# First layer's recurrence on one core: values and gates formed ahead for all tokens, fetched per step by a selection product, temporaries in PSUM, turns of 64 steps

## The chip, the cores and the metric

One core of a Trainium2 chip runs a ten-layer model in one launch. The metric is the device time of the whole launch in microseconds, the median of several executions. The change lies in the first layer, named "cells".

## What is computed

The first layer is a gated matrix recurrence over 1024 tokens of 4 sequences. After x is projected to 128 features, each token gives, for four blocks of 32, a key, a value, a gate (beta), routing logits and one query. The step over time is:

```python
def step(S, inp):                       # S: (batch, 4 blocks, 32, 32)
    logits_t, k_t, v_t, beta_t, q_t = inp
    ...                                 # w: weights of the top 2 of 4 blocks
    kn = k_t / (jnp.linalg.norm(k_t, axis=-1, keepdims=True) + 1e-06)
    retrieved = jnp.einsum('bnij,bnj->bni', S, kn)
    delta = v_t - retrieved
    outer = delta[..., :, None] * kn[..., None, :]
    S_upd = jnp.tanh(beta_t[..., None] * S + outer)
    S_new = (1.0 - w) * S + w * S_upd
    Sq = jnp.einsum('bnij,bj->bni', S_new, q_t)
```

Each step needs the state of the step before, so the 1024 steps run one after another. The other nine layers (a coupling net, a linear recurrence, a binary product, a gated scan, an fp4 feed-forward, RWKV, and local attention in three parts) are not touched.

## The kernel before, in words

The engines run five separate instruction streams, tied by one counting semaphore per layer and engine; `e.after(label)` is a wait for the operation that was recorded with `e.did(label)`, and `back=1` means that operation's instance in the previous turn. Each stream is in order, so the order of the code is the order of the work on that engine.

State. S of one step is a tile of 128 partitions (4 sequences x 32 values of j) by 128 columns (4 blocks x 32 values of i), held in `big7` in two copies used in turn. The sum over j of the delta rule goes over the 32 partitions of a sequence, so it is a product with a constant matrix, `negblock32`, on TensorE. S is never multiplied by the next key after it is complete. Its two parts are: S_new times next key is (1-w) next key S, called kS and made by GpSimd from the state before, plus (w next key) tanh(arg), called kT and made by VectorE from tanh.

Per step s the streams do this.
- TensorE, `cells_tensor`, lines 504 to 544: kS product (L510) and kT product (L514) are added to the bank of step s, in which the value product of the step already stands; then the read-out of the state before (L501), the value product of the next step (L471), one logits product for the gates (L481; every fourth step also a bias product, L479), and a bf16 product whose result nobody reads (L543). Float32 products show as two matmul records and two weight loads each.
- VectorE, `cells_vector`, L770 to L825: outer = bank x key (L775), arg = outer + bS (L778), kT (L811) and wT (L812) from tanh, the new S = wT + aS (L820), bS = S x gate of the next step (L825). bS, outer, arg, T, wT and aS are tiles of `big7`, 128 x 128 float32. Between arg and kT it copies keys, weights, queries and read-outs of half a turn in small pieces, one in each of steps 1 to 7 and 17 to 23 (L724 to L750).
- ScalarE, `cells_scalar`, L598 to L615: tanh (L604); every fourth step it repeats four steps' tokens 32 times over the columns (`repeat_x`, L588), which is the stationary operand of the value and logits products, and makes the gates of four steps by sigmoid (L614).
- GpSimd, `cells_pool`, L873 to L891: kS (L882) and aS (L883), both as soon as the S of the step before is there.

The loop is unrolled by 32 steps, with 32 turns. Products of steps alternate between banks 0 and 2, the gates' logits between banks 5 and 6, the read-outs of half a turn lie in banks 4 and 7. Ahead of the loop VectorE works out routing weights and normed keys (L633 to L713), then ScalarE forms the first turn's repeated tokens and gates (L591 to L597). "staged" is the label of the memset at L713 that frees `big7` for the state.

Of the kernel before, what the change touches and what calls it, by code (L numbers as in the profile page):

```python
# [21 lines left out]
ALU = mybir.AluOpType  # L22
# [130 lines left out]
STEPS = 32  # L153
PARTS = 1
HALF_STEPS = STEPS // 2
CELL_TURNS = SEQ // STEPS
NB = BLK // PARTS
HALF = NB * NST
# [109 lines left out]
class Core:  # L268


    def __init__(self, nc, ctx, ins, out, places, known, found, layers):
# [9 lines left out]
        self.b = [sb(f"big{n}", [P, TOK + (BATCH * STEPS if n == 0 else 0)]) for n in range(9)]  # L281
# [129 lines left out]
def cells_buffers(core):  # L411
    b = core.b
    st = core.b[7]
    cut = lambda a, n: st[:, a:a + n]
    return dict(
        xp=b[0], kn=b[1], wt=b[2], knext=b[3], qd=b[4], lg=b[5], ex=b[6], tmp=b[7], sq=b[8],
        xrep=b[5].rearrange("p (s c) -> p s c", c=P), beta=b[6].rearrange("p (s c) -> p s c", c=P),
        kn_c=cut(0, 128).rearrange("p (n s) -> p n s", n=4), w_c=cut(128, 128).rearrange("p (n s) -> p n s", n=4),
        om_c=cut(256, 128).rearrange("p (n s) -> p n s", n=4), qd_c=cut(384, 128),
        S=[cut(512, 128), cut(640, 128)], aS=cut(768, 128), bS=cut(896, 128), kT=cut(1024, 128),  # L420
        kS=[cut(1664, 128), cut(1792, 128)],
        **{k: cut(at, 128).rearrange("p (n s) -> p n s", n=4) for k, at in (("kw_c", 1920), ("ko_c", 2048), ("knext_c", 2176))},
        outer=cut(1152, 128), arg=cut(1280, 128), T=cut(1408, 128), wT=cut(1536, 128),
        out_bank=[core.bank[4], core.bank[7]],
    )
# [12 lines left out]
def cells_tensor(core, e):  # L438
# [24 lines left out]

    G = STEPS // 4
    logit_bank = [core.bank[5], core.bank[6]]

    def values(s, label):


        for h in range(PARTS):  # L470
            mm = nc.tensor.matmul(core.bank[s % 2 * 2 + h][:, 0:HALF], u["xrep"][:, s, :], w("wv", h * HALF, HALF),  # L471
                                  start=True, stop=False, skip_group_check=True)
        mm.then_inc(*e.did(label))

    def logits(g, m):

        bank = logit_bank[g % 2]
        if m == 0:
            nc.tensor.matmul(bank, core.half[:, TILE:TILE + P], core.half[:, 0:TILE], start=True, stop=False,  # L479
                             skip_group_check=True)  # L480
        return nc.tensor.matmul(bank[:, m * P:(m + 1) * P], u["xrep"][:, 4 * g + m, :], w("wbeta"),  # L481
                                start=False, stop=m == 3, skip_group_check=True)


    pe.wait_ge(*e.after("staged"))
    pe.wait_ge(*e.after("lexp"))
    for g in range(G):
        pe.wait_ge(*e.after("xrep0", g))
        if g >= 2:
            pe.wait_ge(*e.after("beta0", g - 2))  # L490
        for m in range(4):
            mm = logits(g, m)
        mm.then_inc(*e.did(("logits0", g)))
    pe.wait_ge(*e.after("beta0", G - 1))
    pe.wait_ge(*e.after("coefficients"))
    values(0, ("v0",))
# [6 lines left out]

    with e.turns("time", SEQ // STEPS):
        for s in range(STEPS):

            at = lambda x, h: x[:, h * HALF:(h + 1) * HALF]
            pe.wait_ge(*(e.after("kS", s - 1) if s else e.after("kS", STEPS - 1, back=1)))
            for h in range(PARTS):
                nc.tensor.matmul(core.bank[s % 2 * 2 + h][:, 0:HALF], core.c("negblock32"),  # L510
                                 at(u["kS"][(s - 1) % 2], h), start=False, stop=False, skip_group_check=True)
            for h in range(PARTS):
                pe.wait_ge(*(e.after("kT", s - 1, h) if s else e.after("kT", STEPS - 1, h, back=1)))
                nc.tensor.matmul(core.bank[s % 2 * 2 + h][:, 0:HALF], core.c("negblock32"),  # L514
                                 at(u["kT"], h), start=False, stop=True,
                                 skip_group_check=True).then_inc(*e.did(("delta", s, h)))
            if s > 0:
                pe.wait_ge(*e.after("S", s - 1, PARTS - 1))
            else:
                pe.wait_ge(*e.after("S", STEPS - 1, PARTS - 1, back=1))  # L520
# [6 lines left out]
            read_out((s - 1) % STEPS, ("Sq", (s - 1) % STEPS))  # L527
            if s >= 1:
                pe.wait_ge(*e.after("outer", s - 1, PARTS - 1))
            else:  # L530
                pe.wait_ge(*e.after("outer", STEPS - 1, PARTS - 1, back=1))
            if (s + 1) % 4 == 0:
                pe.wait_ge(*(e.after("xrep", (s + 1) // 4, back=1) if s + 1 < STEPS else e.after("xrep", 0)))
            values((s + 1) % STEPS, ("v", (s + 1) % STEPS))

            g, m = (s // 4 - 1) % G, s % 4
            if m == 0:
                pe.wait_ge(*e.after("xrep", g, back=int(s < 4)))
                pe.wait_ge(*e.after("beta", (g - 2) % G, back=int(s < 8)))
            mm = logits(g, m)  # L540
            if m == 3:
                mm.then_inc(*e.did(("logits", g)))
            nc.tensor.matmul(core.bank[1][:, 0:2 * P], core.half[:, 0:P], core.half[:, 0:2 * P], start=True, stop=True,  # L543
                             skip_group_check=True)
    pe.wait_ge(*e.after("S", STEPS - 1, PARTS - 1))
    read_out(STEPS - 1, "Sq_last")

    for label in [("beta", G - 1), ("out_last",)]:
        pe.wait_ge(*e.after(*label))
# [14 lines left out]
def cells_scalar(core, e):  # L564
# [11 lines left out]
    for t in range(TILES):  # L576
        bank, label = core.drain(e, core.to_act)
        nc.scalar.activation(u["tmp"][:, tok(t)], bank, ACT.Sqrt).then_inc(*e.did(label))
        core.found.at[("cells", "knorm", t)] = core.found.at[("cells", *label)]
    act.wait_ge(*e.after("lmax"))  # L580
# [4 lines left out]
    def repeat_x(g, start, label, turn=None):  # L585
        src = u["xp"][:, start:start + TOK].rearrange("p (b t) -> p t b", b=BATCH)
        src = src[:, 0:4, :] if turn is None else src[:, bass.ds(turn * STEPS, 4), :]
        nc.scalar.activation(u["xrep"][:, 4 * g:4 * g + 4, :].rearrange("p s (b j) -> p s b j", b=BATCH),  # L588
                             src.unsqueeze(3).broadcast_to([P, 4, BATCH, 32]), ACT.Copy).then_inc(*e.did(label))

    for g in range(G):  # L591
        repeat_x(g, 4 * g, ("xrep0", g))
    for g in range(G):
        act.wait_ge(*e.after("logits0", g))
        nc.scalar.activation(u["beta"][:, 4 * g:4 * g + 4, :].rearrange("p s c -> p (s c)"),  # L595
                             core.bank[5 + g % 2], ACT.Sigmoid).then_inc(*e.did(("beta0", g)))
    nc.scalar.preload_act_table(ACT.Sigmoid)  # L597
    with e.turns("time", SEQ // STEPS) as turn:  # L598
        for s in range(STEPS):
            for h in range(PARTS):  # L600
                act.wait_ge(*e.after("arg", s, h))
                if s % 4 == 3 and h == PARTS - 1:
                    act.wait_ge(*(e.after("v", s)))
                nc.scalar.activation(u["T"][:, h * HALF:(h + 1) * HALF], u["arg"][:, h * HALF:(h + 1) * HALF],  # L604
                                     ACT.Tanh).then_inc(*e.did(("T", s, h)))
            if s % 4 == 3:

                g = s // 4
                repeat_x(g, STEPS + 4 * g, ("xrep", g), turn)
            if s % 4 == 0:  # L610
                g = (s // 4 - 2) % G
                act.wait_ge(*e.after("bS", 4 * g + 3, back=int(s < 8)))
                act.wait_ge(*e.after("logits", g, back=int(s < 4)))
                nc.scalar.activation(u["beta"][:, 4 * g:4 * g + 4, :].rearrange("p s c -> p (s c)"),  # L614
                                     core.bank[5 + g % 2], ACT.Sigmoid).then_inc(*e.did(("beta", g)))  # L615
    act.wait_ge(*e.after("out_last"))
    for t in range(TILES):
        nc.scalar.activation(u["tmp"][:, tok(t)], u["sq"][:, tok(t)], ACT.Sigmoid).then_inc(*e.did(("osig", t)))
# [7 lines left out]
def cells_vector(core, e):  # L626
    nc, dve, u = core.nc, e.eng, cells_buffers(core)
    tt, G = nc.vector.tensor_tensor, STEPS // 4
# [18 lines left out]
    nc.vector.memset(u["xp"][:, TOK:], 0.0).then_inc(*e.did("xp_pad"))  # L647
# [119 lines left out]
    with e.turns("time", CELL_TURNS) as turn:  # L767
        after, back_one = ((turn + 1) % CELL_TURNS) * STEPS, ((turn + CELL_TURNS - 1) % CELL_TURNS) * STEPS
        first, second = bass.ds(after, HALF_STEPS), bass.ds(turn * STEPS + HALF_STEPS, HALF_STEPS)
        for s in range(STEPS):  # L770
# [8 lines left out]
            if s == 1:  # L779
                copy_key(1, second)  # L780
# [2177 lines left out]
```

## Time and profile before

| | us |
|---|---|
| median of 3 runs | 9550.41 |
| lowest, highest | 9549.36, 9557.72 |
| the profiled execution, its own time | 9542.88 |
| its span in the profile | 9541.1 |
| TensorE busy (matmul) | 7287.1 (76%) |
| VectorE busy | 6764.2 (71%) |
| ScalarE busy | 3257.0 (34%) |
| GpSimd busy | 3224.7 (34%) |

In the rows below, times are microseconds from the start of the span unless marked ns. PE is TensorE's matmul, PEld its weight load, DVE VectorE, ACT ScalarE, POOL GpSimd. L775 is line 775 of the kernel. Full clock is PEclk 1 (2.4 GHz), half clock 0.5 (1.2 GHz). "banks" is PSUM, "big" the big tiles in SBUF. PEclk is the granted TensorE clock as a share of 2.4 GHz. The time of a group of instructions is its busy time; what it means for the span shows only in the order of time.

### The profile page before, as it was taken

The page shows a single profiled execution, that of the slowest core. Times are in us where ns is not written, and L with a number is a line of the kernel's source. Part 1 is how long each engine was busy: PE and PEld are TensorE (multiplying, and loading weights), DVE is VectorE, ACT ScalarE, POOL GpSimd, SP SyncE. Part 2 cuts the span into 40 slices and gives each one's busy share as a digit, 9 for nine tenths or more (in the row PEclk, how much of TensorE's full clock was granted, in tenths as well). Part 3 has the DMA queues.
Part 4 walks back from the last instruction along what each step waited for, and adds up shares of the span by engine and source line. Part 5 has one row for each costly group of instructions (what it writes and reads, how often), then busy time and mean ns, then how long its engine had stood idle before and what let it go on. Part 6 is the DMA issues. An engine that isn't in the chain of part 4 may idle for free. (4 is left out here: it accounts for less than half of the span.)

```text
span 9541.1 us, 245537 instructions
## 1 busy us (share of the span) xinstructions
PE 7287.1 (76%) x92569; PEld 4453.7 (47%) x92569; DVE 6764.2 (71%) x15000; ACT 3257.0 (34%) x5970; POOL 3224.7 (34%) x3982
## 2 busy tenths in 40 slices
PE   4888888888874826656845768888888888888887
PEld 3666666666621212223223345545455545454554
DVE  7777777777758475765485557777777777777776
ACT  2222222222243313223413334444444444444444
POOL 1333333333300000210040035555555555555553
PEclk7888888888887867656865779999999999999999
DMA  0000000000000000000000031111111111111111
GB/s 18 1 1 1 1 1 1 1 1 1 1 5 1 15 0 0 0 0 1 0 0 1 1 120 54 53 53 54 48 56 51 54 51 51 56 51 56 51 56 57
DMA packets 156976, 243.21 MB, mean 25 GB/s; under 512 B 21617, under 2 KB 136849, under 8 KB 150161
## 3 DMA queue, kind: packets, MB, share of 16 engines
q1 hardware_dynamic: 155920, 228.84, 7.8%
q8 instruction: 699, 11.45, 0.5%
q14 instruction: 357, 2.92, 0.1%
HBM read 187.06 MB, written 13.66 MB: 21 GB/s over the span
## 5 line engine op out<-in xcount | busy, mean ns | idle before, releaser
L2751 POOL TENSOR_TENSOR big<-big 128x512 f32<-128x512 f32 x776 | 1040.1, 1373 | 278.4 <-DMA big<-norms 270.7
L2741 POOL TENSOR_TENSOR big<-big 128x512 f32<-128x512 f32 x388 | 494.7, 1275 | 1819.8 <-DVE big L2583 1819.8
L882 POOL TENSOR_TENSOR big<-big 128x128 f32<-128x128 f32 x1024 | 518.3, 506 | 1569.7 <-DVE big L820 1567.4
L604 ACT ACTIVATE big<-big 128x128 f32<-128x128 f32 x1024 | 316.8, 309 | 1902.0 <-DVE big L778 1876.8
L1856 POOL TENSOR_TENSOR small<-big 128x480 f32<-128x480 f32 (+14 forms) x240 | 220.9, 954 | 2187.2 <-ACT big L1614 1866.5
L2158 PE MATMUL banks<-hidden,big 128*128 128x256 f32 x3104 | 828.9, 401 | 111.8 <-DVE big L2583 41.1
L514 PE MATMUL banks<-big,constants_on_chip 128*128 128x128 f32 x2048 | 533.3, 347 | 409.8 <-DVE big L811 408.2
L337 PE MATMUL banks<-big,constants_on_chip 128*128 128x512 f32 (+15 forms) x1088 | 533.5, 644 | 355.2 <-DVE big L1747 191.3
L337 PE MATMUL banks<-big,weights_even 128*128 128x512 f32 (+5 forms) x1152 | 620.5, 692 | 235.0 <-DVE big L1137 45.1
L2222 PE MATMUL banks<-big,hidden 128*32 128x512 f32 x6144 | 770.5, 600 | 4.1 <-ACT big L2473 4.1
L2201 PEld LDWEIGHTS banks<-big 32*32 32x32 f32 x49152 | 535.2, 103 | 471.8 <-issue 471.1
L2201 PE MATMUL banks<-big 32*32 32x64 f32 (+1 forms) x49152 | 659.3, 222 | 87.0 <-issue 86.8
L2158 PEld LDWEIGHTS banks<-hidden,big 128*128 128x128 f32 x3104 | 557.7, 193 | 295.3 <-issue 61.1
L2240 PE MATMUL banks<-big 128*32 128x128 f32 x12160 | 442.0, 301 | 292.6 <-DVE big L2628 274.2
L2473 ACT ACTIVATE big<-banks 128x512 f32<-128x512 f32 x768 | 456.1, 596 | 540.7 <-PE banks L2222 540.4
L514 PEld LDWEIGHTS banks<-big,constants_on_chip 128*128 128x128 f32 x2048 | 352.5, 215 | 564.1 <-DVE big L811 562.5
L2741 POOL TENSOR_TENSOR big<-small 128x512 f32<-128x512 f32 x388 | 498.1, 1284 | 211.8 <-DVE small L2583 211.8
L2240 PEld LDWEIGHTS banks<-big 128*32 128x32 f32 x12160 | 376.8, 121 | 395.2 <-issue 321.0
L471 PE MATMUL banks<-weights_even,big 128*128 128x128 f32 x2050 | 560.7, 361 | 0.7 <-ACT big L595 0.7
L337 PEld LDWEIGHTS banks<-big,constants_on_chip 128*128 128x128 f32 x1088 | 246.7, 252 | 640.8 <-DVE big L1747 215.1
L811 DVE TENSOR_TENSOR big<-big 128x128 f32<-128x128 f32 x1024 | 299.2, 292 | 329.9 <-ACT big L604 313.1
L778 DVE TENSOR_TENSOR big<-big 128x128 f32<-128x128 f32 x1024 | 498.1, 486 | 35.4
(349 smaller groups left out, 15896.3 us busy)
## 6 DMA issues: line engine op xcount, KB each, us to landing
big<-norms SPq DMA_DIRECT2D x776, 128.0 KB, 2.9
big<-qk SPq DMA_DIRECT2D x50, 512.0 KB, 4.8
big<-vo SPq DMA_DIRECT2D x25, 1024.0 KB, 5.8
weights_odd<-ffn SPq DMA_DIRECT2D x25, 537.5 KB, 4.6
hidden<-big SPq DMA_DIRECT2D x171, 64.0 KB, 12.9
hidden<-big SPq DMA_DIRECT2D x25, 256.0 KB, 3.8
hidden<-big SPq DMA_DIRECT2D x25, 255.8 KB, 4.0
big<-pairs SPq DMA_DIRECT2D x6, 1024.0 KB, 10.4
```

The lines of the kernel that those rows point to most:

```text
L337: mm = self.nc.tensor.matmul(bank[0:rows, 0:cols], w, x, start=n == 0, stop=n == len(pairs) - 1)
L471: mm = nc.tensor.matmul(core.bank[s % 2 * 2 + h][:, 0:HALF], u["xrep"][:, s, :], w("wv", h * HALF, HALF), start=True, stop=False, skip_gro ...
L514: nc.tensor.matmul(core.bank[s % 2 * 2 + h][:, 0:HALF], core.c("negblock32"), at(u["kT"], h), start=False, stop=True, skip_group_check=Tru ...
L778: tt(cut(u["arg"], h), cut(u["outer"], h), cut(u["bS"], h), ALU.add).then_inc(*e.did(("arg", s, h)))
L882: nc.gpsimd.tensor_tensor(full(u["kS"][s % 2]), full(S), by(u["ko_c"]), ALU.mult).then_inc(*e.did(("kS", s)))
L2158: mm = self.nc.tensor.matmul(bank[:, n * QTOK:(n + 1) * QTOK], u["w" + name.lower()][:, (2 * g + n) * P:(2 * g + n + 1) * P], u["xs"][:, a ...
L2201: mm = self.nc.tensor.matmul(place[b][32 * c:32 * c + 32, gi, win, skip:], Q[rows, g, half, at:at + WIN], K[rows, g, half, at + skip:at + ...
L2222: mm = self.nc.tensor.matmul(bank[32 * c:32 * c + 32, :], u["xs"][:, at:at + WIN], u["vo"][:, c], start=True, stop=True)
L2240: mm = self.nc.tensor.matmul(u["out_bank"][32 * win:32 * win + 32, jj * P:(jj + 1) * P], u["probT"][jj][:, 4 * g + win, n, :], u["slots"][ ...
L2473: self.nc.scalar.activation(u["slots"][(4 * n + win) % SLOTS], u["value_banks"][win % 2], ACT.Copy).then_inc(*e.did(("kept", f, jj, win)))
L2741: self.nc.gpsimd.tensor_tensor(dst, cos, sin, ALU.add).then_inc(*e.did(("turned_pair", f, name, g)))
L2751: self.nc.gpsimd.tensor_tensor(x, x, u["norms"][:, n, g].unsqueeze(1).broadcast_to([P, 2, QTOK]), ALU.mult).then_inc(*e.did(("scaled", f, ...
```

## The change

1. `STEPS` is 64: 16 turns.
2. Ahead of the loop TensorE forms values and gate logits of all 4096 tokens, 16 products of 32 tokens x 128 to a bank, eight banks of each. ScalarE copies the values to `big3` and the sigmoid of the logits to `big5`. The result has (sequence, 32 steps) on the partitions, one 128-column tile for each half turn.
3. ScalarE spreads the identity to `own` (128 x 4096 columns): for each of 32 steps a 128 x 128 matrix that picks that step's token of each sequence and repeats it over 32 partitions. In the loop one product of `own` and a half turn's values and gates, 256 columns side by side (`vb`), puts both into the bank of the step. It replaces the value product, the logits product, the bias product and the bf16 product L543, and `repeat_x` and the sigmoids in the loop.
4. VectorE multiplies S by the gate straight from columns 128 to 255 of the step's bank. TensorE waits for that multiplication ahead of the kS product.
5. outer and wT lie in bank 2, arg and T in bank 3.
6. The half-turn copies move from VectorE to ScalarE, behind the tanh of steps 2 to 8 and 34 to 40. Two small operations (1 - w, and w x next key) stay on VectorE.
7. The copy of the keys shifted by one token goes; ScalarE reads the keys themselves one column further.

```diff
-STEPS = 32
-PARTS = 1
+STEPS = 64
...
-        outer=cut(1152, 128), arg=cut(1280, 128), T=cut(1408, 128), wT=cut(1536, 128),
+        step_bank=core.bank[0:2], outer=core.bank[2][:, 0:128], wT=core.bank[2][:, 128:256],
+        arg=core.bank[3][:, 0:128], T=core.bank[3][:, 128:256], out_bank=[core.bank[4], core.bank[7]],
...
+    def all_tokens(bank, weight, g, start):
+        for m in range(4):
+            for b in range(BATCH):
+                at = b * SEQ + (4 * g + m) * HALF_STEPS
+                mm = nc.tensor.matmul(bank[32 * b:32 * b + 32, m * P:(m + 1) * P], u["xp"][:, at:at + HALF_STEPS], weight,
+                                      start=start, stop=True, skip_group_check=True)
+        return mm
...
+    def value_and_beta(s, label):
+        nc.tensor.matmul(u["step_bank"][s % 2][:, 0:2 * P], u["own"][:, s % HALF_STEPS, :], u["vb"][s // HALF_STEPS], start=True, stop=False, skip_group_check=True).then_inc(*e.did(label))
...
+            before, back = (s - 1) % STEPS, {} if s else {"back": 1}
+            bank = u["step_bank"][s % 2][:, 0:P]
+            pe.wait_ge(*e.after("kS", before, **back))
+            pe.wait_ge(*e.after("bS", s, **back))
+            nc.tensor.matmul(bank, core.c("negblock32"), u["kS"][before % 2], start=False, stop=False, skip_group_check=True)
+            pe.wait_ge(*e.after("kT", before, **back))
+            nc.tensor.matmul(bank, core.c("negblock32"), u["kT"], start=False, stop=True,
+                             skip_group_check=True).then_inc(*e.did(("delta", s)))
+            pe.wait_ge(*e.after("S", before, **back))
...
+            read_out(before, ("Sq", before))
+            pe.wait_ge(*e.after("outer", before, **back))
...
+            value_and_beta((s + 1) % STEPS, ("v", (s + 1) % STEPS))
...
+    ident = core.c("ident").rearrange("p (b s) -> p s b", b=BATCH).unsqueeze(3).broadcast_to([P, HALF_STEPS, BATCH, 32])
+    copy(u["own"].rearrange("p s (b j) -> p s b j", b=BATCH), ident, "own")
+    act.wait_ge(*e.after("beta_kept", TILES - 1))
+    copy(u["vb"][0][:, 0:P], u["v"][:, 0:P])
+    copy(u["vb"][0][:, P:2 * P], u["beta"][:, 0:P], "vb_first")
...
+            dve.wait_ge(*e.after("delta", s))
+            tt(cut(u["outer"]), cut(u["step_bank"][s % 2][:, 0:P]), spread(u["kn_c"], s), ALU.mult).then_inc(
+                *e.did(("outer", s)))
...
+            tt(u["arg"], u["outer"], u["bS"], ALU.add).then_inc(*e.did(("arg", s)))
...
+            tt(new, u["wT"], u["aS"], ALU.add).then_inc(*e.did(("S", s)))
+            dve.wait_ge(*e.after("v", ahead))
+            dve.wait_ge(*e.after("S", s))
+            tt(u["bS"], new, u["step_bank"][ahead % 2][:, P:2 * P], ALU.mult).then_inc(*e.did(("bS", ahead)))
```

## Rows read from the trace of the kernel before

**Rows 1.** Groups by line of the time loop: names, shapes, count, busy us, mean ns, idle.

```profile
L604 ACT ACTIVATE big<-big 128x128 f32<-128x128 f32 x1023 | 316.5, 309 | 1900.0 <-DVE big L778 1874.7 <-PE banks L471 14.7 <-PE banks L481 10.6
...
L811 DVE TENSOR_TENSOR big<-big 128x128 f32<-128x128 f32 x1023 | 298.9, 292 | 329.5 <-ACT big L604 312.6
...
L775 DVE TENSOR_TENSOR big<-banks,big 128x128 f32<-128x128 f32 x1024 | 291.6, 285 | 151.5 <-issue 85.2 <-PE banks L514 63.0
...
L775 DVE TENSOR_TENSOR big<-banks,big x1024: 281/283/293, 164.4 to 2639.2; 128x128 f32<-128x128 f32 x171
```

**Rows 2.** Timeline of one step at full clock: start us, duration us, engine, line.

```profile
1501.32 0.30 PEld L471 LDWEIGHTS banks<-weights_even,big 128*128 128x128 f32 x2
...
1501.54 0.30 PEld L481 LDWEIGHTS banks<-weights_even,big 128*128 128x128 f32 x2
1501.60 0.41 POOL L883 TENSOR_TENSOR big<-big 128x128 f32<-128x128 f32 x1
1501.61 0.54 DVE L778 TENSOR_TENSOR big<-big 128x128 f32<-128x128 f32 x1
...
1501.88 0.30 PEld L510 LDWEIGHTS banks<-big,constants_on_chip 128*128 128x128 f32 x2
...
1502.19 0.31 ACT L604 ACTIVATE big<-big 128x128 f32<-128x128 f32 x1 [1.50 <-DVE big L778]
1502.53 0.29 DVE L811 TENSOR_TENSOR big<-big 128x128 f32<-128x128 f32 x1 [0.38 <-ACT big L604]
1502.74 0.28 DVE L812 TENSOR_TENSOR big<-big 128x128 f32<-128x128 f32 x1
...
1502.88 0.49 PE L514 MATMUL banks<-big,constants_on_chip 128*128 128x128 f32 x2 [0.50 <-DVE big L811]
1503.06 0.29 DVE L820 TENSOR_TENSOR big<-big 128x128 f32<-128x128 f32 x1
1503.38 0.29 DVE L825 TENSOR_TENSOR big<-big 128x128 f32<-128x128 f32 x1
...
1503.59 0.28 DVE L775 TENSOR_TENSOR big<-banks,big 128x128 f32<-128x128 f32 x1
```

**Rows 3.** Stretches: us, busy of PE, PEld, DVE, ACT, POOL, then PEclk, DMA, GB/s.

```profile
50.00:149.00 99.00, 0.00 (x0) 0.00 (x0) 97.03 (x58) 3.62 (x1) 0.00 (x0) 0.50 0.00 0
...
400.00:2600.00 2200.00, 1803.47 (x10230) 1485.91 (x10231) 1683.47 (x5854) 509.29 (x1363) 814.01 (x1876) 0.87 0.00 1
...
4308.00:4350.00 42.00, 30.70 (x278) 20.09 (x277) 15.21 (x39) 11.00 (x25) 0.00 (x0) 0.50 0.00 0
```

**Rows 4.** Timeline of steps at half clock.

```profile
204.28 0.29 DVE L775 TENSOR_TENSOR big<-banks,big 128x128 f32<-128x128 f32 x1 [0.66 <-PE banks L514]
...
204.61 0.29 DVE L778 TENSOR_TENSOR big<-big 128x128 f32<-128x128 f32 x1
...
204.94 0.31 ACT L604 ACTIVATE big<-big 128x128 f32<-128x128 f32 x1 [2.00 <-DVE big L778]
...
205.32 0.55 PEld L510 LDWEIGHTS banks<-big,constants_on_chip 128*128 128x128 f32 x2
...
205.75 0.55 PEld L514 LDWEIGHTS banks<-big,constants_on_chip 128*128 128x128 f32 x2
...
243.19 0.80 PE L514 MATMUL banks<-big,constants_on_chip 128*128 128x128 f32 x2 [1.79 <-DVE big L811]
...
244.03 0.29 DVE L775 TENSOR_TENSOR big<-banks,big 128x128 f32<-128x128 f32 x1
```

**Rows 5.** Timeline of VectorE over the end of a turn.

```profile
238.67 0.29 DVE L825 TENSOR_TENSOR big<-big 128x128 f32<-128x128 f32 x1
241.85 0.29 DVE L775 TENSOR_TENSOR big<-banks,big 128x128 f32<-128x128 f32 x1 [2.89 <-issue]
```

**Rows 6.** Timeline ahead of the loop.

```profile
149.66 4.26 ACT L588 ACTIVATE big<-big 128x512 f32<-128x512 f32 x8 [67.80 <-DVE big L713]
...
164.43 0.29 DVE L775 TENSOR_TENSOR big<-banks,big 128x128 f32<-128x128 f32 x1 [11.25 <-PE banks L514]
```

More of the change, by code:

```diff
@@ L280, in __init__ @@
         self.x = sb("hidden", [P, TOK])
-        self.b = [sb(f"big{n}", [P, TOK + (BATCH * STEPS if n == 0 else 0)]) for n in range(9)]
+        self.b = [sb(f"big{n}", [P, TOK + int(n == 1)]) for n in range(9)]
         self.const_at, n = columns(constants())
@@ L462, in cells_tensor @@
         core.product(e, core.to_act, [(core.c("block32"), u["tmp"][:, tok(t)])])
[L464 to L482, printed above, removed]
@@ L485, in cells_tensor @@
[L485 to L488, printed above, removed]
-        if g >= 2:
[L490 to L496, printed above, removed]
+    for k in range(core.to_act.filled - 4, core.to_act.filled):
+        pe.wait_ge(*e.after("drained", "to_act", core.to_act.phase, k))
@@ new lines, in all_tokens @@
+    def all_tokens(bank, weight, g, start):
[5 more added lines that the diff above has]
+        return mm
+    for g in range(TILES):
+        if g >= 2:
+            pe.wait_ge(*e.after("v_kept", g - 2))
+        all_tokens(core.bank[g % 2], w("wv"), g, True).then_inc(*e.did(("v_all", g)))
@@ new lines, in cells_tensor @@
+    for g in range(TILES):
+        if g >= 2:
+            pe.wait_ge(*e.after("beta_kept", g - 2))
+        bank = core.bank[2 + g % 2]
+        nc.tensor.matmul(bank, core.half[:, TILE:TILE + P], core.half[:, 0:TILE], start=True, stop=False,
+                         skip_group_check=True)
+        all_tokens(bank, w("wbeta"), g, False).then_inc(*e.did(("beta_all", g)))
+    def value_and_beta(s, label):
+        nc.tensor.matmul(u["step_bank"][s % 2][:, 0:2 * P], u["own"][:, s % HALF_STEPS, :], u["vb"][s // HALF_STEPS], start=True, stop=False, skip_group_check=True).then_inc(*e.did(label))
@@ L502, in read_out @@
                          start=True, stop=True, skip_group_check=True).then_inc(*e.did(label))
-    with e.turns("time", SEQ // STEPS):
-        for s in range(STEPS):
[L507 to L520, printed above, removed]
+    pe.wait_ge(*e.after("vb_first"))
+    pe.wait_ge(*e.after("own"))
+    pe.wait_ge(*e.after("coefficients"))
+    value_and_beta(0, "v_first")
+    with e.turns("time", CELL_TURNS):
+        for s in range(STEPS):
+            before, back = (s - 1) % STEPS, {} if s else {"back": 1}
[7 more added lines that the diff above has]
+            pe.wait_ge(*e.after("S", before, **back))
             if s == 1:
@@ L526, in cells_tensor @@
                 pe.wait_ge(*e.after("out", 1))
[L527 to L545, printed above, removed]
+            read_out(before, ("Sq", before))
+            pe.wait_ge(*e.after("outer", before, **back))
+            if s + 1 == HALF_STEPS:
+                pe.wait_ge(*e.after("vb", 1))
+            if s + 1 == STEPS:
+                pe.wait_ge(*e.after("vb", 0))
+            value_and_beta((s + 1) % STEPS, ("v", (s + 1) % STEPS))
+    pe.wait_ge(*e.after("S", STEPS - 1))
     read_out(STEPS - 1, "Sq_last")
-    for label in [("beta", G - 1), ("out_last",)]:
-        pe.wait_ge(*e.after(*label))
+    pe.wait_ge(*e.after("bS", 0))
+    pe.wait_ge(*e.after("out_last"))
     for t in range(TILES):
@@ L579, in cells_scalar @@
         core.found.at[("cells", "knorm", t)] = core.found.at[("cells", *label)]
+    for g in range(TILES):
+        act.wait_ge(*e.after("v_all", g))
+        nc.scalar.activation(u["v"][:, tok(g)], core.bank[g % 2], ACT.Copy).then_inc(*e.did(("v_kept", g)))
     act.wait_ge(*e.after("lmax"))
     nc.scalar.activation(u["ex"][:, 0:TOK], u["lg"][:, 0:TOK], ACT.Exp).then_inc(*e.did("lexp"))
-    act.wait_ge(*e.after("staged"))
[L585 to L596, printed above, removed]
+    for g in range(TILES):
+        act.wait_ge(*e.after("beta_all", g))
+        if g == 0:
+            act.wait_ge(*e.after("lexp"))
+        nc.scalar.activation(u["beta"][:, tok(g)], core.bank[2 + g % 2], ACT.Sigmoid).then_inc(*e.did(("beta_kept", g)))
@@ L597, in cells_scalar @@
+    copy(u["vb"][0][:, P:2 * P], u["beta"][:, 0:P], "vb_first")
+    act.wait_ge(*e.after("coefficients"))
     nc.scalar.preload_act_table(ACT.Sigmoid)
-    with e.turns("time", SEQ // STEPS) as turn:
+    with e.turns("time", CELL_TURNS) as turn:
+        after, earlier_turn = ((turn + 1) % CELL_TURNS) * STEPS, ((turn + CELL_TURNS - 1) % CELL_TURNS) * STEPS
         for s in range(STEPS):
[L600 to L615, printed above, removed]
@@ new lines, in cells_scalar @@
+            act.wait_ge(*e.after("arg", s))
+            nc.scalar.activation(u["T"], u["arg"], ACT.Tanh).then_inc(*e.did(("T", s)))
+            h = 0 if s >= HALF_STEPS else 1
+            start = after if h == 0 else turn * STEPS + HALF_STEPS
+            chore = s % HALF_STEPS
+            if chore == 2:
+                copy_steps("w_c", "wt", h, start, ("w_c", h))
+            if chore == 3:
+                copy_steps("knext_c", "kn", h, start, ("knext_c", h))
+            if chore == 4:
+                copy_steps("kn_c", "kn", h, start, ("kn_c", h))
@@ new lines, in cells_scalar @@
+            if chore == 5:
+                act.wait_ge(*e.after("Sq", HALF_STEPS - 1 if h == 0 else STEPS - 1))
+                copy(u["qd_c"][:, h * P:(h + 1) * P], u["qd"][:, bass.ds(start * BATCH, P)], ("qd_c", h))
+            if chore == 6:
+                done = turn * STEPS if h == 0 else earlier_turn + HALF_STEPS
+                keep_out(h, bass.ds(done, HALF_STEPS), ("out", h))
+            if chore == 7:
+                act.wait_ge(*e.after("v", HALF_STEPS - 1 if h == 0 else STEPS - 1, **({"back": 1} if h else {})))
+                copy_tile("v", h, start * BATCH, None)
@@ L616, in cells_scalar @@
+            if chore == 8:
+                copy_tile("beta", h, start * BATCH, ("vb", h))
+    act.wait_ge(*e.after("Sq_last"))
+    keep_out(1, slice(SEQ - HALF_STEPS, SEQ), "out_last")
     act.wait_ge(*e.after("out_last"))
+    act.wait_ge(*e.after("bS", 0))
     for t in range(TILES):
@@ L757, in cells_vector @@
     weigh_next_key(0)
[L758 to L759 removed]
+    e.name_last("coefficients")
     chain()
[L762 to L825 removed]
@@ L874, in cells_pool @@
             S = u["S"][s % 2]
-            for h in range(PARTS):
-                pool.wait_ge(*(e.after("S", s - 1, h) if s else e.after("S", STEPS - 1, h, back=1)))
+            pool.wait_ge(*(e.after("S", s - 1) if s else e.after("S", STEPS - 1, back=1)))
             by = lambda v: v[:, :, s].unsqueeze(2).broadcast_to([P, BLK, NST])
```

167 lines of the change are left out of this document (59 added, 108 removed).

## Prediction

> **What bounds the kernel now.** I read the grouped instructions of the time loop first, then one step of it in order of time, then the granted clock by stretch, a low-clock step, the turn boundary and the stretch ahead of the loop. The loop is L775 to L825, 1024 steps; its first L775 starts at 164.4 us and its last at 2639.2 [rows 1], so it takes 2475 of 9541 us, 2.42 us a step. Nothing else is touched but some 15 us ahead of it.
>
> In a plain step [rows 2] VectorE is the chain. From start to start: kT L811 to wT L812 0.21 (2.53 to 2.74), to the new state S L820 0.32, to bS L825 0.32, to the next outer L775 0.21, to arg L778 0.32 (204.28 to 204.61 [rows 4]), to tanh on ScalarE L604 0.58 (1501.61 to 1502.19), and to kT 0.34: 2.30 us. TensorE's part lies beside it: L514 starts 0.34 after kT starts, its record takes 0.49 and ends at 1503.37, and L775 starts only at 1503.59, because VectorE was still making wT, S and bS. So TensorE has 0.2 us to spare. The earlier product of the sum, L510 on kS, ran at 1501.88, a microsecond ahead of kT. And L778, both inputs in SBUF, takes 0.54 beside GpSimd's L883, where L775, one input in PSUM, takes 0.28. Without GpSimd beside it L778 takes 0.29 (at 204.61), and ScalarE follows 0.33 after its start [rows 4].
>
> Check: 1023 x 2.30 = 2353; 31 turn ends add 3.18 - 0.21 = 2.97 each, less 0.25 for an L778 that runs with GpSimd still idle there [rows 5]: 84; the 38 us left of 2475 are steps at the lower TensorE clock, where TensorE's queue of products is the bound (L775 waits 0.66 for L514) [rows 4]. The clock averages 0.87 over the loop [rows 3], that is 2.4 GHz for about three quarters and 1.2 for the rest.
>
> **The change, part by part.**
> 1. *The wait on bS.* Values and gates come into one bank per step: columns 0 to 127 take the value and the two negative products, columns 128 to 255 the gate, which VectorE reads while it forms bS(s). So TensorE, in step s, now waits for bS(s) ahead of the kS product. bS(s) is VectorE's last operation of step s-1. Before, TensorE needed only kT there, three operations earlier. Behind this wait stand kS, kT, the read-out and the next selection product; VectorE waits for the kS and kT products at L775. What was beside the chain is now in it: from bS start to TensorE's start 0.34 (as from L811 at 1502.53 to L514 at 1502.88 [rows 2]); the kS product holds the array 0.22 at 2.4 GHz (L471's weights at 1501.32, L481's at 1501.54); the kT product 0.49; to L775 0.04. That is 1.09 us where there was 0.21. GpSimd's kS(s-1) is made a step ahead, so it is not late.
> 2. *The same at 1.2 GHz.* Weights load to weights load 0.43 (205.32 to 205.75), the lone product 0.80 (243.19) and L775 at 244.03 [rows 4]: 0.34 + 0.43 + 0.80 + 0.04 = 1.61 us.
> 3. *L778 without GpSimd.* arg to tanh falls from 0.58 to 0.33. GpSimd's second operation ends at 1502.01, and the S that released it began 2.30 before the one at 1503.06, at 1500.76 [rows 2]: it is done by S + 1.25; arg now comes at S + 0.32 + 1.09 + 0.32 = 1.73 or later, so this 0.25 is gained whether or not PSUM operands help. It is the whole gain of part "temporaries in PSUM"; L811, L812, L820 and L825 at 0.28 to 0.29 have nothing to give back [rows 1].
> 4. *PSUM operands.* A PSUM source on VectorE costs 285 ns against 292 with both in SBUF (L775, L811 [rows 1]); below, nothing to lose. Four dependent operations now read or write PSUM in new ways (arg, kT with wT, S, bS), and no row writes a 128x128 tile there from VectorE. Lower bound 0; upper, the 0.25 that a hindered operation of this size shows, each, 4 x 0.25 x 1023 = 1023 us. I take 0, as L775 is the nearest row; the far end stays outside the range, since nothing here comes near it. The Trainium skill, "VectorE: DVE Perf Modes", section on the TRN2 errata, puts a PSUM source 62 cycles of 0.96 GHz, some 65 ns, above an SBUF source; by it, an estimate, the sum below would be 4 x 0.065 x 1023 = 266 us higher. Here L775 against L811 does not bear it out.
> 5. *TensorE's other work.* Gone from each step: value and logits products (0.22 each), the bias product every fourth, and the idle-filling bf16 product L543. Added: one selection product of 256 columns, twice the 0.22 of 128, 0.44. It runs after kT's and is needed a step later: nothing on the path. But TensorE works less: at 2.4 GHz three products of 0.22, one of 0.44 and a tail of 0.27 are 1.4 us of a 2.94 us step, 47%, where the loop now shows 82% busy [rows 3]. At 1.2 GHz twice that, 2.6 of 3.46, 75%. A stretch at 4308 us with TensorE 73% busy (30.70 of 42.00) was granted 0.50 throughout [rows 3], while at 205 us, in a low stretch of this loop after which the clock rose, the products follow each other without a pause (weights at 205.32 and 205.75, each load 0.55 [rows 4]). So I take 1.2 GHz for the loop.
> 6. *Chores.* VectorE's copies move to ScalarE, seven after a tanh in each 32 steps, with those of v and beta. They go into ScalarE's 1900 us of idle time ahead of L604 [rows 1]: 0. ScalarE's sixteen 0.6 us operations per 32 steps (L588, L614) go, also from idle time. TensorE's waits for them come eight steps later and more.
> 7. *Turns.* 15 ends instead of 31. VectorE resumes 3.18 after the last bS start (238.67 to 241.85 [rows 5]); TensorE would now release it after 1.61 anyway, so an end costs 1.57: 24 us in all.
> 8. *Ahead of the loop.* 256 small products (56 us at 0.22) and their 16 evacuations lie under VectorE's work from 50 to 149 us, with TensorE idle [rows 3]. After "staged" (149.66) ScalarE spreads the identity, 4096 columns, 4.26 as the eight of L588 with 512 each, copies two tiles, 0.5, and TensorE needs 0.05 + 0.87 + 0.43 + 0.80 + 0.04: first L775 at 156.6 instead of 164.4 [rows 6]: -8. If the cover were gone it would cost up to 56 + 10.
>
> **The sum.** A step: 0.21 + 0.32 + 0.32 + 1.61 + 0.32 + 0.33 + 0.34 = 3.45; with 0.01 of rounding 3.46. Loop 1023 x 3.46 + 24 = 3564, +1089 on 2475. The profiled execution took 9542.9: 9542.9 + 1089 - 8 = 10,624. The median of the three runs lies 7.5 above it; so 10,631, said as 10,630.
>
> **Rivals.**
> *Full clock.* Same chain, but the clock stays at 2.4 GHz: step 2.94, turn end 3.18 - 1.09 = 2.09; 1023 x 2.94 + 31 = 3039, +564 - 8: 10,106. For it: the before loop holds that clock three quarters of the time. Against: what part 5 says. A mix of both levels lies between. The Trainium skill, "TensorE: Matmul & The Clock Gate", section "Why this matters for your kernels", says that a drop comes from idle gaps between bursts of matmuls; a loop that gives TensorE products in every step would stay at 2.4 GHz, this rival. The trace speaks against it: the loop gives products in every step and still has 0.87.
> *PSUM operands dear.* With 0.06 us on each of the four operations of part 4, a fifth of their 0.29: + 246, 10,876. Against: L775.
> *Faster.* If the two products behind bS cost less than 0.46 from bS start to outer start (0.21 + the 0.25 of part 3), the step shrinks; if VectorE never waits for TensorE, it is 2.05: 1023 x 2.05 + 15 x 2.97 = 2142, -333 - 8, 9,209. The place is L775's wait, the price 0.25 a step. For it: TensorE has 0.2 to spare today. Against: the lone kT product takes 0.49 by itself. It needs the new wait to be met early, that is not to do what it says.
>
> **How the numbers follow.** Half clock 0.70 (its own range 10,480 to 10,760, a tenth of a us a step either way), full or mixed clock 0.17, PSUM dear 0.06, faster 0.05, and 0.02 that products and gain cancel. The range 10,080 to 10,800 takes in the first two, less their tails. A measurement of this kernel can tell 0.2% from no change. Slower 0.93, same 0.02, faster 0.05.
>
> **What would show it.** L775 released by TensorE's kT product in all steps, idle some 1.3 us before it; the kS product's weights load released by VectorE's bS; arg about 0.29; PEclk 5 in the loop's slices; 15 idle pieces put down to issue; the first L775 near 157. The prediction is wrong if bS to outer is under 0.5 us, if the clock stays high, or if arg, T or wT are slower than 0.35.

## The result and the profile after

| | before | changed |
|---|---|---|
| median, us | 9554.06 (4 runs) | 10675.17 (4 runs) |
| lowest, highest | 9549.36, 9563.18 | 10666.19, 10680.68 |
| profiled execution, span | 9541.1 | 10675.2 |
| loop: first outer (L775, now L755) to the last | 2474.7 | 3531.4 |

The ratio is 1.117, 95% interval 1.115 to 1.119: 12% slower. The page of the changed kernel, its 40 slices of 267 us:

```profile
span 10675.2 us, 238749 instructions
...
PE   5777777777777775447567466888888888888887
...
DVE  6444444444444556666755845777777777777676
...
PEclk6555555555555587667567568999999999999999
```

The loop is slices 2 to 14 (its first steps are in slice 1). VectorE, at 7 before, is at 4, and the granted clock is 5 in all of them. The two operations of VectorE that matter most have new lines: outer (the product of the step's bank with the key) is now L755 and bS (the new state times the next gate) is L778. The source view of L755 answers to the last line of [rows 1], and the stretch of the loop to [rows 3] (columns as there):

```profile
L755 DVE TENSOR_TENSOR banks<-banks,big x1024: 298/299/300, 156.2 to 3687.6; 128x128 f32<-128x128 f32 x171
its engine sat idle before it (us, times) until:
  PE banks L507: 1331.5, 1009
  PE banks L487: 42.1, 15
```

```profile
156.00:3688.00 3532.00, 2561.42 (x8188) 1823.81 (x8188) 1722.96 (x6204) 315.04 (x1247) 800.39 (x2078) 0.50 0.00 0
```

In every one of the 1024 steps VectorE waits for TensorE before outer; 1009 of these waits last 1.32 us in the mean and end with the kT product L507. The kernel before had 63 us of such waits in all. One step in order of time answers to [rows 2]:

```profile
1504.14 0.29 DVE L767 TENSOR_TENSOR big<-banks,big 128x128 f32<-128x128 f32 x1 [0.33 <-ACT banks L596]
1504.35 0.29 DVE L768 TENSOR_TENSOR banks<-banks,big 128x128 f32<-128x128 f32 x1
1504.67 0.29 DVE L775 TENSOR_TENSOR big<-banks,big 128x128 f32<-128x128 f32 x1
1505.00 0.29 DVE L778 TENSOR_TENSOR big<-big,banks 128x128 f32<-128x128 f32 x1
...
1505.34 0.80 PE L505 MATMUL banks<-big,constants_on_chip 128*128 128x128 f32 x2 [0.92 <-DVE big L778]
...
1505.72 0.55 PEld L507 LDWEIGHTS banks<-big,constants_on_chip 128*128 128x128 f32 x2
1505.93 0.63 PE L507 MATMUL banks<-big,constants_on_chip 128*128 128x128 f32 x2
...
1506.60 0.30 DVE L755 TENSOR_TENSOR banks<-banks,big 128x128 f32<-128x128 f32 x1 [1.32 <-PE banks L507]
...
1506.94 0.30 DVE L758 TENSOR_TENSOR banks<-banks,big 128x128 f32<-128x128 f32 x1
```

From the start of bS (L778, 1505.00) to the start of outer (L755, 1506.60) it is 1.60 us, where [rows 2] has 0.21. In it lie 0.34 until TensorE starts the kS product (L505), and both products, the kT product (L507) ending at 1506.56. arg (L758) takes 0.30 where L778 of before took 0.54. The step from one L755 (1503.18) to the next is 3.42.

The next two lines are the end of the first turn on VectorE, as in [rows 5]:

```profile
374.13 0.29 DVE L778 TENSOR_TENSOR big<-big,banks 128x128 f32<-128x128 f32 x1
377.43 0.30 DVE L755 TENSOR_TENSOR banks<-banks,big 128x128 f32<-128x128 f32 x1 [3.02 <-PE banks L487]
```

It is 3.30 from bS to outer here, and 3.02 of it idle. There are 15 such ends, with 42.1 us of idle time in all, 2.81 each. The view puts it down to TensorE's selection product L487, and in [rows 1] the 31 ends, 85.2 us or 2.75 each, to nothing ("issue"); since an end idles as long as before, the wait is taken to be VectorE's own resuming here too.

The span grew by 1134.1 us: the loop by 1056.7, the start of the loop moved by -8.2 (156.2 for 164.4), and **85.6 us lie behind the loop, in code that the change does not touch**. They are in the local attention layer. One VectorE operation comes once in each of its 24 turns; its source view gives the first and the last start, for the kernel before and for the changed one:

```profile
L2691 DVE TENSOR_SCALAR heads<-heads x24: 170/171/173, 5731.3 to 9425.5; 128x6 f32 x24
```

```profile
L2636 DVE TENSOR_SCALAR heads<-heads x24: 170/171/172, 6775.8 to 10559.7; 128x6 f32 x24
```

23 turns take 3694.2 us before and 3783.9 after, 89.7 more: 160.6 and 164.5 us a turn (some of the expectations below use 160.4 and 163.9; the medians of this view's turns are 160.3 and 164.1). From the last outer of the loop to the first of these operations it is 3092.1 us before and 3088.2 after, so the layers between are not slower.

### The profile page after: what moved, and what is told of

The parts are those of the page before. It is cut to its first block and busy times, and to the rows that moved or that the text cites. A ratio compares the mean times of both kernels' runs of the same rounds, so it can differ in the third digit from the quotient of the medians.

```text
span 10675.2 us, 238749 instructions
## 1 busy us (share of the span) xinstructions
PE 7912.1 (74%) x89689; PEld 4648.5 (44%) x89689; DVE 6581.5 (62%) x14613; ACT 3003.9 (28%) x5686; POOL 3107.8 (29%) x3950
## 3 DMA queue, kind: packets, MB, share of 16 engines
q14 instruction: 318, 2.61, 0.1%
## 5 line engine op out<-in xcount | busy, mean ns | idle before, releaser
L505 PE MATMUL banks<-big,constants_on_chip 128*128 128x128 f32 x2048 | 815.7, 502 | 970.6 <-DVE big L778 970.6
L487 PE MATMUL banks<-big 128*128 128x256 f32 x2050 | 1230.7, 704 | 59.7 <-ACT big L570 59.7
L505 PEld LDWEIGHTS banks<-big,constants_on_chip 128*128 128x128 f32 x2048 | 514.5, 312 | 1708.4 <-DVE big L778 1708.2
L830 POOL TENSOR_TENSOR big<-big 128x128 f32<-128x128 f32 x1024 | 415.3, 406 | 2733.5 <-DVE big L775 2733.1
L596 ACT ACTIVATE banks<-banks 128x128 f32<-128x128 f32 x1024 | 268.3, 262 | 3217.9 <-DVE banks L758 3217.9
L755 DVE TENSOR_TENSOR banks<-banks,big 128x128 f32<-128x128 f32 x1024 | 306.5, 299 | 1373.5 <-PE banks L507 1331.5
L2103 PE MATMUL banks<-hidden,big 128*128 128x256 f32 x3104 | 875.5, 417 | 126.6 <-issue 44.6
L2103 PEld LDWEIGHTS banks<-hidden,big 128*128 128x128 f32 x3104 | 584.2, 202 | 328.1 <-issue 116.0
L2185 PE MATMUL banks<-big 128*32 128x128 f32 x12160 | 466.2, 307 | 254.4 <-DVE big L2573 219.2
L507 PE MATMUL banks<-big,constants_on_chip 128*128 128x128 f32 x2048 | 649.7, 421 | 0.0
L487 PEld LDWEIGHTS banks<-big 128*128 128x128 f32 x2050 | 560.1, 333 | 60.0 <-ACT big L570 60.0
L492 PEld LDWEIGHTS banks<-big 128*128 128x128 f32 x2050 | 559.9, 333 | 1.3 <-DVE big L775 1.3
```

The lines of the kernel that those rows point to most:

```text
L487: nc.tensor.matmul(u["step_bank"][s % 2][:, 0:2 * P], u["own"][:, s % HALF_STEPS, :], u["vb"][s // HALF_STEPS], start=True, stop=False, sk ...
L492: nc.tensor.matmul(bank[:, c:c + BATCH], u["S"][(s + 1) % 2], u["qd_c"][:, s * BATCH:(s + 1) * BATCH], start=True, stop=True, skip_group_c ...
L505: nc.tensor.matmul(bank, core.c("negblock32"), u["kS"][before % 2], start=False, stop=False, skip_group_check=True)
L507: nc.tensor.matmul(bank, core.c("negblock32"), u["kT"], start=False, stop=True, skip_group_check=True).then_inc(*e.did(("delta", s)))
L2103: mm = self.nc.tensor.matmul(bank[:, n * QTOK:(n + 1) * QTOK], u["w" + name.lower()][:, (2 * g + n) * P:(2 * g + n + 1) * P], u["xs"][:, a ...
L2185: mm = self.nc.tensor.matmul(u["out_bank"][32 * win:32 * win + 32, jj * P:(jj + 1) * P], u["probT"][jj][:, 4 * g + win, n, :], u["slots"][ ...
```

## The experiments

**1. The gate in its own bank, so no wait on bS.**

```diff
-        nc.tensor.matmul(u["step_bank"][s % 2][:, 0:2 * P], u["own"][:, s % HALF_STEPS, :], u["vb"][s // HALF_STEPS], start=True, stop=False, skip_group_check=True).then_inc(*e.did(label))
+        own, vb = u["own"][:, s % HALF_STEPS, :], u["vb"][s // HALF_STEPS]
+        nc.tensor.matmul(u["step_bank"][s % 2][:, 0:P], own, vb[:, 0:P], start=True, stop=False, skip_group_check=True)
+        nc.tensor.matmul(u["gate_bank"][s % 2][:, 0:P], own, vb[:, P:2 * P], start=True, stop=True, skip_group_check=True).then_inc(*e.did(label))
...
-            pe.wait_ge(*e.after("bS", s, **back))
...
-            tt(u["bS"], new, u["step_bank"][ahead % 2][:, P:2 * P], ALU.mult).then_inc(*e.did(("bS", ahead)))
+            tt(u["bS"], new, u["gate_bank"][ahead % 2][:, 0:P], ALU.mult).then_inc(*e.did(("bS", ahead)))
```

The gate's banks are 5 and 6, used in turn.

> The changed kernel, but the gate goes by a product of its own into another bank (5 or 6), so TensorE's kS product no longer waits for bS. Theory (the wait puts both products into the chain, the low clock makes them dearer): bS to outer falls from 1.60 to 0.21 us; VectorE's chain alone is then 0.21 + 0.32 + 0.33 + 0.21 + 0.33 + 0.33 + 0.29 = 2.02 us a step; at 1.2 GHz TensorE's queue of five products of 0.43 and the wait for S make some 2.26. Loop 1023 x 2.02 to 2.26 + 45 = 2110 to 2360 instead of 3531, total 9,255 to 9,505. Rival (PSUM temporaries or the selection product itself are what costs): the step stays near 3.4 and the time near 10,600.

9267.5 us, ratio to before 0.967 (0.966 to 0.969). Its loop, and a step in it:

```profile
157.00:2320.00 2163.00, 1846.54 (x10221) 1552.96 (x10221) 1655.16 (x6197) 314.78 (x1246) 799.63 (x2076) 0.85 0.00 1
```

```profile
1500.40 0.29 DVE L779 TENSOR_TENSOR big<-big,banks 128x128 f32<-128x128 f32 x1
...
1500.60 0.29 DVE L756 TENSOR_TENSOR banks<-banks,big 128x128 f32<-128x128 f32 x1
```

The 1.60 is 0.20 again and a plain step is 2.02 (the median of the 1023). Everything else of the change is still in, so PSUM temporaries, selection products and long turns are not what costs. With the gate in its own bank and the wait gone the change would have been a gain of 3%. No run keeps both in one bank without the wait, so what sharing a bank costs apart from the wait is not shown.

**2. The wait on bS alone, in the kernel before.**

```diff
+            pe.wait_ge(*e.after("bS", s, **({} if s else {"back": 1})))
             for h in range(PARTS):
                 nc.tensor.matmul(core.bank[s % 2 * 2 + h][:, 0:HALF], core.c("negblock32"),
```

> The kernel before with one line added: TensorE waits for bS(s) ahead of the kS product. Nothing else of the change. Theory: step 3.46 us at 1.2 GHz (0.21 + 0.32 + 0.32 + 1.61 + 0.33 + 0.33 + 0.34), loop 1023 x 3.46 + 31 x 1.57 = 3588, total 10,656; if its extra products keep the clock at 2.4 GHz, step 2.93 and total 10,130. Rival (the wait is harmless): 9,550.

10,679 us in one run: one line does what the whole change did.

```profile
165.00:3760.00 3595.00, 2882.75 (x11512) 2353.50 (x11512) 1761.10 (x6586) 574.89 (x1535) 906.30 (x2110) 0.50 0.00 0
```

```profile
1501.83 0.29 DVE L826 TENSOR_TENSOR big<-big 128x128 f32<-128x128 f32 x1
...
1502.18 0.79 PE L511 MATMUL banks<-big,constants_on_chip 128*128 128x128 f32 x2 [0.31 <-DVE big L826]
...
1503.43 0.29 DVE L776 TENSOR_TENSOR big<-banks,big 128x128 f32<-128x128 f32 x1 [1.31 <-PE banks L515]
```

bS to outer is again 1.60 (L826 to L776), the median step 3.45. And the clock is 0.50 although the logits, the bias and the idle-filling product are all still there, with TensorE 80% busy (2882.75 of 3595). It fell at the start of the loop, in stretches of 10 us:

```profile
160.00:170.00 10.00, 7.56 (x59) 6.66 (x57) 2.61 (x11) 5.05 (x9) 0.87 (x2) 1.00 0.01 2
170.00:180.00 10.00, 6.80 (x33) 5.89 (x34) 5.46 (x23) 1.93 (x5) 2.62 (x6) 0.65 0.00 1
180.00:190.00 10.00, 8.21 (x35) 6.77 (x35) 5.11 (x20) 0.98 (x5) 2.91 (x7) 0.50 0.01 2
```

The products are those of the kernel before, step for step, and only the step is longer. So the longer step alone brings the clock down; that the change takes products out is not needed for it.

**3. The changed kernel with TensorE's clock fed.**

```diff
+            for _ in range(3):
+                nc.tensor.matmul(u["step_bank"][(s + 1) % 2][:, 0:512], core.half[:, 0:P], core.half[:, 0:512], start=True,
+                                 stop=True, skip_group_check=True)
             value_and_beta((s + 1) % STEPS, ("v", (s + 1) % STEPS))
```

> The changed kernel with three bf16 products of 512 columns per step, whose result nobody reads, ahead of the selection product, in time in which TensorE waits. Theory (half of the loss is the clock): granted clock 1.0 in the loop, bS to outer 1.09 instead of 1.60, step 3.42 - 0.51 = 2.91, loop 1023 x 2.91 + 32 = 3009, total 10,155. Rival (the clock does not follow the work, or the products do not get faster): 10,677.

10,109 us, 46 less than forecast, in one run. TensorE's idle-filling products are L523, the selection product is still L487, bS is now L781 and outer L758.

```profile
156.00:3206.00 3050.00, 2032.63 (x11253) 1323.10 (x11252) 1721.90 (x6201) 315.16 (x1247) 801.20 (x2078) 0.98 0.00 1
```

```profile
1501.04 0.29 DVE L781 TENSOR_TENSOR big<-big,banks 128x128 f32<-128x128 f32 x1 [0.68 <-PE banks L487]
...
1502.13 0.30 DVE L758 TENSOR_TENSOR banks<-banks,big 128x128 f32<-128x128 f32 x1 [0.80 <-PE banks L507]
```

At a clock of 0.98 bS to outer is 1.09, as the prediction had it for 2.4 GHz, and the loop takes 3050 us. Of the 1057 us that the loop lost, the clock is 481 (3531 - 3050) and the two products in series, with all that the change gains against them, 576. (The loop was forecast at 3009. In the turns' medians the first three steps take 3.42, 4.07 and 3.55 us where most others take 2.91: 2.3 us more in a turn, 16 times. In 30 steps of the loop bS waits for the selection product behind the three fillers, as the first row shows, 20.3 us in all.)

**4. The changed kernel with TensorE's code moved by 172 instructions.**

```diff
+    for _ in range(86):
+        nc.tensor.matmul(core.bank[5][:, 0:32], core.half[:, 0:P], core.half[:, 0:32], start=True, stop=True,
+                         skip_group_check=True)
     pe.wait_ge(*e.after("vb_first"))
```

> The changed kernel with 86 small bf16 products (172 instructions) added to TensorE's stream ahead of the time loop, where TensorE is idle. The changed kernel is 86 us slower than the loop explains; the 24 turns of the local attention layer, whose code is the same, take 163.9 instead of 160.4 us each. The stream of TensorE is 1365 instructions longer than before; with 172 more it is 1537, six times 256 plus one. Theory (where the turn's code lies decides where TensorE stalls for instructions): turns back at 160.4 us, total 10,592. Rival (something else that the first layer leaves behind): turns at 163.9, total 10,677.

10,623.6 us in one run, 52 less than the changed kernel; forecast was 85.

```profile
L2639 DVE TENSOR_SCALAR heads<-heads x24: 170/171/172, 6775.6 to 10508.3; 128x6 f32 x24
```

3732.7 us for 23 turns, 162.3 a turn: more than half of the way back, with a loop as long as the changed kernel's (3531.1). Work that runs 6 ms earlier, beside the path, made a later layer faster. The rest did not go, so bringing TensorE's offset back near a multiple of 256 was not enough. The streams of the other engines had moved too, VectorE's by some 450 instructions, and no run moves them alone.

**5. The kernel before with the temporaries in PSUM.**

```diff
-        outer=cut(1152, 128), arg=cut(1280, 128), T=cut(1408, 128), wT=cut(1536, 128),
+        **{k: core.bank[3][:, n * 128:(n + 1) * 128] for n, k in enumerate(("outer", "wT", "arg", "T"))},
```

> The kernel before with one part of the change alone: outer, arg, T and wT in PSUM (bank 3), nothing else. Theory (in the kernel before, arg with both inputs in SBUF is held up by GpSimd; a PSUM input frees it; elsewhere PSUM costs nothing): L778 0.30 instead of 0.54, arg to tanh 0.33, step 2.02, loop 1023 x 2.02 + 31 x 2.97 = 2158 instead of 2475, total 9,235. Rival (PSUM operands give nothing): 9,560.

9275.9 us, ratio 0.971 (0.969 to 0.973).

```profile
1501.30 0.29 DVE L775 TENSOR_TENSOR banks<-banks,big 128x128 f32<-128x128 f32 x1
...
1501.61 0.40 POOL L883 TENSOR_TENSOR big<-big 128x128 f32<-128x128 f32 x1
...
1501.63 0.30 DVE L778 TENSOR_TENSOR banks<-banks,big 128x128 f32<-128x128 f32 x1
```

arg runs at 0.30 in the very place where [rows 2] has 0.54, beside GpSimd's L883. The plain step is 2.02, the loop 2207 instead of 2475. The forecast of 2158 missed 49: every fourth step is 2.10 (ScalarE's tanh has one more wait there in the code), and the second and third step of a turn take 2.61 and 2.23.

This one line gains 2.9%, and experiment 1, with all the rest of the change, 3.3%. The rest shortens the loop by another 42 us (2165 for 2207), of which the local attention layer takes back some (162.9 for 160.9 us a turn).

**6. Experiment 1 with the clock fed.** One bf16 product of 256 columns per step ahead of the selection products, otherwise as the first.

> The first experiment (gate in its own bank, no wait on bS) with one bf16 product of 256 columns per step, whose result nobody reads. The first experiment took 2165 us for the loop at a clock of 0.85. Theory (its steps of 2.14 to 2.27 are those at 1.2 GHz): clock near 1.0, loop 1023 x 2.01 + 15 x 2.85 = 2099, total 9,200. Rival (more work in TensorE's queue only lengthens it): 9,270 or more.

9224.5 us, ratio 0.965 (0.963 to 0.967).

```profile
157.00:2293.00 2136.00, 1744.32 (x11254) 1372.97 (x11254) 1642.37 (x6203) 315.16 (x1247) 803.01 (x2077) 0.97 0.01 2
```

Clock 0.97 for 0.85, and the loop 29 us shorter; 66 were forecast. In the median of the turns eight of the 64 steps are still longer than 2.10: the first two of a turn (2.14 and 2.35), and six that lie nine steps apart (2.12 to 2.26). What holds them was not followed.

**7. The changed kernel with the temporaries back in SBUF.** The cuts of `big7` for the four tiles, nothing else.

> The changed kernel with outer, arg, T and wT back in SBUF. Theory (with the wait in place GpSimd is done before arg is formed, so PSUM gives there only the faster tanh, 0.26 instead of 0.31): step 3.42 + 0.05 = 3.46, arg 0.29, loop 3580, total 10,720. Rival (PSUM is what keeps arg short here): arg 0.54, step 3.67, total 10,930.

10,715 us, in one run.

```profile
1501.16 0.29 DVE L758 TENSOR_TENSOR big<-big 128x128 f32<-128x128 f32 x1
1501.82 0.29 DVE L767 TENSOR_TENSOR big<-big 128x128 f32<-128x128 f32 x1 [0.37 <-ACT big L596]
```

arg has two SBUF inputs again and still takes 0.29: GpSimd is long done. The total was forecast at 10,720. So under the wait on bS the move to PSUM is worth 0.03 us a step (3.45 for 3.42), where it is worth 0.28 in the kernel before.

**8. The kernel before with TensorE's code moved by some 86 instructions.** 42 products like those of the fourth, and four waits, ahead of the wait for "staged".

> The kernel before with 42 small bf16 products and four waits (some 86 instructions) added to TensorE's stream ahead of the time loop, where TensorE is idle: the offset, counted in TensorE's instructions less whole multiples of 256, that the change gives to the layers behind it. Theory (TensorE's code position alone makes most of the 86 us): a local attention turn of 162 to 164 us instead of 160.4, total 9,580 to 9,640. Rival (it takes the other engines' offsets, or something else): 160.4 and 9,550.

9618.2 us, in one run, 62 more than the kernel before.

```profile
L2696 DVE TENSOR_SCALAR heads<-heads x24: 170/171/172, 5726.4 to 9499.2; 128x6 f32 x24
```

3772.8 us for 23 turns, 164.0 a turn, where the time loop is unchanged (2474). In this kernel the position of TensorE's code alone makes 78.6 of the 89.7 us that the changed kernel's 23 turns had more.

**9. Experiment 6 with the offset chosen.** 29 idle products ahead of the loop.

> The version with the gate in its own bank and the clock fed, with 29 small bf16 products (58 instructions) more in TensorE's stream ahead of the time loop. In the runs so far with the changed kernel's VectorE code, a turn of the local attention layer took 163.9, 162.1, 162.4, 162.5 and 160.7 us at TensorE offsets (instructions against the kernel before, less multiples of 256) of 82, 254, 27, 152 and 210. This one has 210. Theory (the offset sets the turn): turn 160.7, 24 x 1.8 = 43 us less, total 9,182. Rival (the offset does not carry over from one kernel to another): turn 162.5, total 9,225.

9187.0 us, ratio 0.9595 (0.958 to 0.961): faster than both kernels, 4% under the kernel before.

```profile
L2643 DVE TENSOR_SCALAR heads<-heads x24: 170/171/172, 5381.9 to 9065.2; 128x6 f32 x24
```

3683.3 us for 23 turns, 160.1 a turn, for 162.5 in the sixth. In this one case the turn of a kernel could be forecast from the turn of another with the same offset (160.7 forecast).

## Why the prediction was right

The forecast was 10,630 by the half-clock case; measured 10,675, in the range of 10,080 to 10,800, and in that case's own of 10,480 to 10,760. The mechanism was right: the wait was in every step, as long as forecast. Two things were luck: how the clock was argued (part 5), and that a term that the sum did not have was in part made up for by others.

- *Parts 1 and 2, the wait on bS.* 1.61 forecast for bS to outer at 1.2 GHz, 1.60 measured; 1.09 and 1.09 at 2.4 GHz (experiment 3). Experiments 1 and 2 show it from both sides: without the wait the step is 2.02, with the wait alone 3.45.
- *Part 3, arg without GpSimd.* 0.30. That it is gained whether or not PSUM operands help was shown by experiment 7, and that PSUM gives it by itself where GpSimd still runs, by experiment 5.
- *Part 4, PSUM operands.* 0 was taken; an outer or arg that lands in PSUM takes 299 ns where SBUF took 292 or less, and tanh, with both operands in PSUM, 262 where it took 309. From the start of tanh to that of kT it is 0.29 for 0.34, which the sum did not have: that is why the step is 3.42 and not 3.46. The 65 ns per PSUM source that come out of the Trainium skill's "VectorE: DVE Perf Modes", section on the TRN2 errata, are not seen in any of the four operations: from outer to arg it is 0.34 (1506.60 to 1506.94), where it was 0.33 in [rows 4].
- *Part 5, the clock.* 0.50 in the whole loop, as taken. It did not fall there: TensorE had been idle for 60 us ahead of the loop, the clock was at 0.50 when the loop began, at 156 us, and it never rose in it. That more work for TensorE brings it up is shown by experiment 3 (0.98). But the busy shares from which the prediction argued do not decide it: experiment 2 has TensorE 80% busy and was granted 0.50, the kernel before has it 82% busy and was granted 0.87. The comparison with the stretch at 4308 us was a weak step that came out right. The rule of the Trainium skill's "TensorE: Matmul & The Clock Gate", section "Why this matters for your kernels", that idle gaps between bursts of matmuls are what throttles, is not tested by this loop, where nothing fell. Experiment 2 does not bear it out: from 160 to 190 us the clock fell from 1.00 to 0.50 with products in every step, and TensorE never paused for more than 1.45 us.
- *Part 6, chores.* Nothing on the path, as forecast.
- *Part 7, turns.* 4.87 (the median) - 3.42 = 1.45 an end, 1.57 forecast. The forecast took the one end of [rows 5], idle for 2.89, where the mean of the 31 was 2.75.
- *Part 8, ahead of the loop.* 156.2 for 156.6. The spreading of the identity began 0.4 later than taken (150.04) and took 3.62 for 4.26.
- *The sum.* Loop 3531 for 3564, 33 too much: 0.04 in each of 1023 steps, less four steps in each turn that take 3.53 to 3.63, for which the sum had nothing. The start was right. The profiled execution was 10,677 for 10,624. The miss of 53 is the 86 us in the local attention layer, for which the sum had no term, less those 33.

The 86 us are the one thing that the prediction did not see. It said that nothing is touched but the loop and some 15 us ahead of it; the lengths of the instruction streams are touched too. Offsets are TensorE's instructions against the kernel before, as counted in the traces, less multiples of 256. Counts of one kernel differ by up to five (experiment 4 rests on a count of 1365 for the changed kernel, which would be an offset of 85, and of 1 for its own kernel). That multiples of 256 may be left out was taken and not tested by itself; the two pairs of kernels that lie a whole multiple apart, 8 and the changed one, 3 and 9, have nearly the same turn.

| kernel | TensorE offset | local attention, us a turn (mean of 23) |
|---|---|---|
| the kernel before | 0 | 160.6 |
| 8, before moved | about 82 | 164.0 |
| 2, before and wait | about 27 | 161.6 |
| 5, before with PSUM temporaries | about -6 | 160.9 |
| the changed kernel | 82 | 164.5 |
| 7, changed with SBUF temporaries | about 81 | 164.3 |
| 4, changed moved | 254 | 162.3 |
| 1, gate in its own bank | 27 | 162.9 |
| 6, the same, clock fed | 152 | 162.5 |
| 3, changed, clock fed | 210 | 160.6 |
| 9, as 6, with the offset chosen | 210 | 160.1 |

At 82 the turn is 164 with either kernel's VectorE code; near 0 and at 27 it differs by 1 to 2 us between them. What in the turn stalls was seen only as more of TensorE's idle time without a releaser. That TensorE waits for its instructions there is the theory of experiment 4; no view shows it. The granted clock is another part of it: over the 23 turns it was 0.97 in the kernel before and 0.98 in experiment 9, 0.96 in experiment 8 and 0.95 in the changed kernel. Whether the stalls lower the clock or the clock has a cause of its own, and what share the other engines' streams have, stays open.

## What to carry to other kernels

When two results share a PSUM bank, ask which reader the next product into it must now wait for, and whether that reader was the last operation of the step: the bank that saves a product here put both of TensorE's products behind VectorE's last operation, and a bank of its own for the gate undid it. Price a product on the path at both clock levels, since a longer step can also lower the clock that its products run at, as in experiment 2. And when a change alters the length of an unrolled stream, compare the layers behind it before the difference is put down to the edit.

## What the runs showed that I had not expected

- The position of TensorE's code moves a later loop by up to 3.4 us in a turn of 161, by nothing but products far ahead whose result nobody reads (experiment 8, 62 us of 9557); experiments 4 and 9 moved it the other way by 2.2 and 2.4 us.
- TensorE, 80% busy over 3595 us, was granted 1.2 GHz in all of them but the first 8 (experiment 2), by nothing but a longer step with the same products.
- VectorE's addition of two SBUF tiles into a third takes 0.54 us beside a GpSimd operation (the kernel before), and 0.30 in the same place when one input and the output lie in PSUM (experiment 5).
- A 128 x 128 tanh from PSUM to PSUM takes 262 ns, from SBUF to SBUF 309.
